# Gathering the first 32 edge blocks from x and looking their factors up by products

## What is computed

```python
def gcn_residual(x, edge_index, edge_weight, W, b, gamma, beta):
    deg = segment_sum(edge_weight, dst) + 1.0
    dinv = rsqrt(deg)
    norm = dinv[src] * edge_weight * dinv[dst]
    agg = segment_sum(norm[:, None] * (x @ W)[src], dst)
    agg = agg + (dinv * dinv)[:, None] * (x @ W)
    h = layernorm(agg + b) * gamma + beta
    return relu(0.5 * h + 0.5 * x)

xn = layernorm(x)
x = x + gcn_residual(xn, ...) + linear_attention(xn, Wq, Wkv, Wproj, bproj)
x = x + mixture_of_experts(layernorm(x))     # 16 experts, top 2
```

## Time and profile before

| | |
|---|---|
| median of three runs | 1661.91 us (1657.16 to 1662.6) |
| profiled execution | 1661.33 us |
| its span | 1659.5 us |
| busy in the span: PE, weight loads, DVE, ACT, POOL | 84%, 73%, 60%, 32%, 61% |
| first and last gather issued | 119.2 and 1105.2 us |

### The profile page before, as it was taken

One profiled execution on the slowest core, in us unless ns is written; L12 is line 12 of the kernel. 1 busy time (PEld: TensorE's weight loads), 2 busy tenths in 40 slices (PEclk: granted clock), 3 DMA queues, 4 the chain that ended last, 5 costly groups with the idle time before them and its releaser, 6 DMA issues. The chain is left out here.

```text
span 1659.5 us, 31767 instructions
## 1 busy us (share of the span) xinstructions
PE 1400.5 (84%) x8109; PEld 1212.2 (73%) x8110; DVE 999.2 (60%) x3840; ACT 525.4 (32%) x1448; POOL 1016.7 (61%) x1074
## 2 busy tenths in 40 slices
PE   5988987697797978787797789775899999999986
PEld 4777876586685867676686677663689999989974
DVE  7766564352774746547575277267655555566668
ACT  1474321121232222212222122013444444444424
POOL 0117777777777777777777777750345554545547
PEclk7889999997899879898899989786899999999998
DMA  8165433333333333333333333328532332254267
GB/s 278 30 201 151 124 106 106 103 105 105 105 105 105 105 105 105 105 106 103 105 105 105 105 105 106 105 74 156 156 121 73 97 100 96 81 170 152 74 232 280
DMA packets 110401, 201.27 MB, mean 121 GB/s; under 512 B 24880, under 2 KB 66480, under 8 KB 110288
## 3 DMA queue, kind: packets, MB, share of 16 engines
q0 software_dynamic: 48240, 131.91, 27.3%
q1 hardware_dynamic: 52704, 58.94, 11.7%
q10 hardware_dynamic: 9344, 9.05, 1.7%
HBM read 166.21 MB, written 33.60 MB: 120 GB/s over the span
## 5 line engine op out<-in xcount | busy, mean ns | idle before, releaser
L144 POOL DMA_INDIRECT ring<-table,src x782 | 748.8, 958 | 261.8 <-issue 221.3
L1273 PE MATMUL bank<-ring,work 128*128 x1756 | 432.3, 402 | 101.5 <-SPq L537 89.5
L1273 PEld LDWEIGHTS bank<-ring,work 128*128 128x128 f32 x1756 | 345.1, 200 | 178.1 <-issue 130.3
L1831 ACT ACTIVATE one<-bank,b 128x128 f32<-128x128 f32 x424 | 155.9, 368 | 217.3 <-PE bank L1858 192.3
L1858 PEld LDWEIGHTS bank<-one,w 128*128 128x128 f32 x1696 | 206.9, 193 | 8.1 <-issue 2.0
L1777 POOL DMA_INDIRECT spread<-y,to_x x109 | 109.1, 1001 | 163.1 <-DMA spread<-y,to_x 78.9
L1858 PE MATMUL bank<-one,w 128*128 128x128 f32 x1696 | 207.8, 276 | 1.2 <-issue 0.7
L1866 PE MATMUL bank<-w,one 128*128 128x256 f32 x848 | 201.5, 381 | 3.5 <-DVE y L1930 3.5
L756 DVE TENSOR_SCALAR work<-work 128x128 f32<-128x128 f32 x686 | 183.6, 365 | 2.0 <-DVE work L753 0.2
L1866 PEld LDWEIGHTS bank<-w,one 128*128 128x128 f32 x848 | 153.1, 191 | 20.5 <-issue 4.0
L774 DVE TENSOR_SCALAR work<-work,dst,w 128x128 f32<-128x128 f32 x192 | 58.2, 364 | 166.4 <-PE bank L1273 121.5
(11 more groups left out here) (303 smaller groups left out, 2136.7 us busy)
## 6 DMA issues: line engine op xcount, KB each, us to landing
w<-in_w SPq DMA_DIRECT2D x32, 512.0 KB, 4.8
ring<-table,src POOLq DMA_INDIRECT x782, 2.8
got<-spread SPq DMA_DIRECT2D x11, 1024.0 KB, 9.2
rows<-xn SPq DMA_DIRECT2D x1, 6272.0 KB, 27.1
out<-xn SPq DMA_DIRECT2D x12, 512.0 KB, 5.3
x<-in_x SPq DMA_DIRECT2D x4, 896.0 KB, 8.7
work<-in_x_cols ACTq DMA_DIRECT2D x28, 128.0 KB, 2.4
work<-in_x_cols SPq DMA_DIRECT2D x21, 128.0 KB, 3.2
```

What stands on the lines that cost most here:

```text
L144: return pool.indirect_dma_start(out=m.ring[:, b % RING, :], out_offset=None, in_=a.table, in_offset=bass.IndirectOffsetOnAxis(ap=m.src[:, ...
L1273: last = nc.tensor.matmul(agg, hot[:, k, :], two[:, k, :], start=False, stop=False)
L1831: act.activation(hT[:, fc, :], up_ps[fc], ACT.Relu, bias=b1[:, fc, bass.ds(i * SLOTS + slot, 1)]).then_inc(h_ok, 1)
```

## The change

The first 32 blocks (`GATHERED_AHEAD`) are gathered from x itself and no longer from the table. POOL does so as soon as the source indices have landed, which SP now loads right after the constants. Their rows lack the factor of their source node, so the factor is multiplied into the edge weights: during batches 2 to 9 DVE builds one-hots of the source's lane (`source_hots`), PE turns them (`sources`), ACT copies them out; DVE builds masks of the source's tile (`masks`). When the factors of all rows are known, DVE splits them into three bf16 parts (`split`), PE multiplies (`looked_up`, four groups of 24 matmuls), and DVE picks and sums (`found`) between the steps of the pair words.

The table's rows are now x times one factor, with no shift, since the weights of the graph layer are centred too. ACT takes the column sums out of PSUM and POOL adds them to the weights after its 32 gathers. The factor is the root of degree times variance in one. ACT scales and stores all tiles of the table, the last eight in two halves behind the lookups.

No keys are done during the histogram. All 49 tiles' keys come after the pair words, and eight tiles are visited among them, after the keys of tiles 1, 3, 9, 16, 23, 30, 37 and 44. The mixing visits 41 tiles and pauses in ten turns instead of five. POOL's gathers from block 32 on wait for the table and, as before, for freed slots. `summed_up` of the last tile comes in the turn after it. The statistics of x are taken two tiles a batch; x_cols are loaded later. The one-hots of the histogram no longer lie in the ring.

```diff
-TAIL = 16
-PAUSES = (8, 16, 24, 32, 40)
+PAUSES = tuple(range(0, 46, 5))
+TWICE = 2
+SOUGHT = 4
+SEEK = 8
...
+            pool.wait_ge(ld_src, 16)
             for b in range(GATHERED_AHEAD):
-                gather(pool, m, a, b).then_inc(landed[b // 4], 16)
+                gather(pool, m, a.x, b).then_inc(landed[b // 4], 16)
+            pool.wait_ge(seek_copied, CSUM_COPIED)
+            for ch in range(DC):
+                for k in range(3):
+                    w = m.weights[:, ch, k * D:(k + 1) * D]
+                    last = pool.tensor_tensor(w, w, csum[:, k * D:(k + 1) * D], ALU.add)
+            last.then_inc(read, 1)
...
+            pool.wait_ge(table_sent, 16 * (FINAL + 2))
             for b in range(GATHERED_AHEAD, FULL):
                 if b >= RING and b % 2 == 0:
                     pool.wait_ge(freed, (b + 2 - RING) // 2 + CREDIT)
-                gather(pool, m, a, b).then_inc(landed[b % RING // 4], 16)
+                gather(pool, m, a.table, b).then_inc(landed[b % RING // 4], 16)
...
-        VISITS_AFTER = {TAIL + 16: 0, TAIL + 23: 1, TAIL + 30: 2}
+        VISITS_AFTER = {1: 0, 3: 1, 9: 2, 16: 3, 23: 4, 30: 5, 37: 6, 44: 7}
...
+            def source_hots(k):
+                g0, g1 = k * SOUGHT // 2, (k + 1) * SOUGHT // 2
+                full = [P, g1 - g0, P, 2]
+                dve.tensor_tensor(src_hots[:, g0:g1], iota2[:, None, :, :].broadcast_to(full),
+                                  src_lo[:, 2 * g0:2 * g1].rearrange("p (g k) -> p g k", k=2)[:, :, None, :].broadcast_to(full),
+                                  ALU.is_equal).then_inc(seek_ok, 1)
...
+            def found(j):
+                b0, b1 = j * SEEK, (j + 1) * SEEK
+                dve.wait_ge(seek_mm, TURNED + 1 + j)
+                c.add(dve.tensor_tensor(sought[:, b0:b1].rearrange("p (g k) n -> p g k n", k=2),
+                                        found_ps[j].rearrange("p (g k) n -> p g k n", k=2),
+                                        src_mask[:, b0 // 2:b1 // 2].rearrange("p g n k -> p g k n"), ALU.mult))
+                c.wait()
+                c.add(dve.reduce_sum(s_edge[:, b0:b1], sought[:, b0:b1], axis=AX.X))
+                c.wait()
+                c.add(dve.tensor_tensor(m.w[:, b0:b1], m.w[:, b0:b1], s_edge[:, b0:b1], ALU.mult))
+                dve.sem_inc(seek_ok, 1)
...
+            for t, end, groups in ((t0, t0 + 4, FOUND // 2), (t0 + 4, t1, FOUND)):
+                act.wait_ge(seek_mm, TURNED + groups)
+                for of in range(t, end):
+                    scaled(of)
+                sent(t, end)
...
+            def looked_up(j):
+                for i in range(SEEK):
+                    b = j * SEEK + i
+                    for part in range(3):
+                        last = nc.tensor.matmul(found_ps[j][:, i, :], src_cols[:, b * P:(b + 1) * P], s_parts[:, part, :],
+                                                start=(part == 0), stop=(part == 2))
+                last.then_inc(seek_mm, 1)
...
-            for t in range(TAIL, NT):
+            pe.wait_ge(seek_ok, LOOKED)
+            pe.wait_ge(read, CENTRED_OK)
+            for t in range(NT):
                 scored(t)
-                context(t - 2)
+                if t >= 2:
+                    context(t - 2)
...
-                if on(t, 1) and not (t == LAST + 1):
+                if on(t, 1):
                     summed_up(t - 1)
```

More of the change, by code:

```diff
@@ L669, in scales @@
-                dve.wait_ge(rstd_ok, len(PARTS) + part)
-                c.add(root(m.dinv[:, t0:t1], var_p[:, t0:t1], seed_p[:, t0:t1], t1 - t0))
-                c.wait()
-                dve.tensor_tensor(row_scale[:, t0:t1], m.dinv[:, t0:t1], rstd[:, t0:t1], ALU.mult)
-                dve.tensor_tensor(row_shift[:, t0:t1], m.dinv[:, t0:t1], shift[:, t0:t1], ALU.mult).then_inc(rstd_ok, 1)
-            def centre():
-                dve.wait_ge(made, CSUM)
-                for k, (w0, n) in enumerate(CENTRED):
-                    for ch in range(DC):
-                        last = dve.scalar_tensor_tensor(m.weights[:, ch, w0:w0 + n], csum_ps[k], -1.0 / D, m.weights[:, ch, w0:w0 + n],
-                                                        ALU.mult, ALU.add)
-                last.then_inc(read, 1)
@@ L683, in _ @@
[L683 to L704 removed]
+                dve.wait_ge(seed_p_ok, SEEDED if part == FINAL else part + 1)
@@ L797, in aggregated @@
                 r.end()
-            between()
+            dve.wait_ge(read, CENTRED_OK)
             c.add(dve.tensor_copy(m.dst[:, 0:NB], dst_i))
@@ L811, in _, with seen @@
             dve.wait_ge(flag_ok, 1)
-            pair_words(dve, c, m, sums_ps, tf, between)
-            keys_to(FLAG_AFTER)
+            steps = iter(range(2 * FOUND + 3))
+            def seen():
+                step = next(steps)
+                if step % 2 == 1 and step // 2 < FOUND:
+                    found(step // 2)
+            pair_words(dve, c, m, sums_ps, tf, seen)
             with dve.If(out_of_order(dve)):
@@ new lines, in _ @@
+            for part in range(FINAL):
+                act.wait_ge(var_p_ok, part + 1)
+                seeds(part, grown, ln_s, seed_p, *DEGREES[part])
+                if part == 0:
+                    act.wait_ge(made, CSUM)
+                    act.activation(csum[:, 0:2 * D], csum_ps[0], ACT.Copy, scale=-1.0 / D)
+                    act.activation(csum[:, 2 * D:3 * D], csum_ps[1], ACT.Copy, scale=-1.0 / D).then_inc(seek_copied, 1)
+                if part == FINAL - 1:
+                    seeds(FINAL, var_p, spread, seed_x, 0, NT)
+                act.wait_ge(scale_ok, part + 1)
+                t0, t1 = DEGREES[part]
+                for t in range(t0, t1):
+                    scaled(t)
+                sent(t0, t1)
@@ new lines, in looked_up @@
+            def looked_up(j):
[4 more added lines that the diff above has]
+                                                start=(part == 0), stop=(part == 2))
+                last.then_inc(seek_mm, 1)
+            for b in range(BATCHES):
+                degrees(b)
+                if 3 <= b < 3 + TURNED:
+                    sources(b - 3)
+                if b == 3 + TURNED:
+                    column_sums()
@@ L1341, in _ @@
             pe.wait_ge(part_read, FINAL + 1)
             to_lanes(FINAL)
-            for t in range(TAIL, NT):
+            pe.wait_ge(ready, 2)
+            pe.wait_ge(var_p_ok, FINAL + 1)
+            for up in range(UP):
+                nc.tensor.matmul(sums_ps, m.ones[0:LOW], deg[:, 2, up::UP], start=(up == 0), stop=(up == UP - 1))
+            nc.tensor.matmul(drops_ps, m.ones, drops[:], start=True, stop=True).then_inc(made, 1)
+            pe.wait_ge(seek_ok, SPLIT)
+            pe.wait_ge(seek_copied, TURNED)
```

373 lines of the change are left out of this document (172 added, 201 removed).

## The result

| | before | changed |
|---|---|---|
| median (range) | 1662.26 us (1657.16 to 1663.57, 4 runs) | 1634.51 us (1633.52 to 1637.61, 4 runs) |
| profiled execution: time, span | 1661.33, 1659.5 us | 1635.0, 1633.2 us |
| first gather from the table, last gather | 119.2, 1105.2 us | 119.70, 1071.2 us |
| last visit ends | 1116.57 us | 1088.78 us |

The ratio is 0.9849 [0.9821, 0.9878]: 1.5% faster; the profiled executions lie 26.3 us apart, the medians 27.8. The forecast of 1625 us was 10 us too low; the time lies in the range of 1608 to 1650.

What follows compares the result with a forecast made beforehand. Serial gather stream on POOL bounds the kernel; last gather at 117 + 945.6 + 5 = 1067.6 us against 1105.2, 37.6 earlier, less 1 for the last sum; 1661.3 - 36.6 = 1624.7, about 1625 us; range 1608 to 1650.

Steps and rivals of the forecast that it cites:

- What bounds the kernel: Whole kernel: one serial stream of indirect gathers on POOL, 1.2625 us each; 986 of 1659.5 us hang on it.
- Part 1: Head: 32 gathers read x during the histogram, at most 1.57 us each, ending at 70 us; 750 left take 945.6 us.
- Rival A: Head is late: gathers crawl beside one-hots, weights come late or small steps grow; first gather about 135, 1643 us; chance 0.15.
- Part 2: Histogram without keys: one-hots end at 86 us against 98.97 (bounds 84 and 99), flag at 95 us against 117.4.
- Part 3: Pair words, lookups, first visit at 116 us, first gather into a freed slot at 117; bounds 115 and 130.
- Part 4: All 49 keys beside eight visits: PE runs against the stream, and POOL waits about 5 us near visit 8.
- Rival B: Keys stage: the ring stays full, a stall of 20 us and not 5, 1640 us; chance 0.14.
- Part 5: Mixing with ten pauses instead of five: PE's chain takes 729 us where the stream needs 824, so pauses stay hidden.
- rival C: Mixing: PE becomes the bound through pauses of 45.2 us with their visit; 1685 us at eight of ten; chance 0.07.
- D: Better than forecast: head at 110 us, no stall, PE not behind at the end, 1612 us; chance 0.09.
- The tail: After the last gather: last visit begins 5 us after its issue, left unchanged; bounds 6 us less, 12 us more.
- The last sum: End of the mixing: the last sum, one turn later, stands beside the last tile's aggregation and costs 1 us.

Runs made afterwards that it cites:

- the repeated run: The changed kernel itself run once more, nothing edited, beside the kernel before at 1662.61 us: 1636.98 us median, ratio 0.9837.
- the second group: Four runs at the usual time (kernel before 1662.61 us): changed kernel again 1636.98, 32 gathers from the table 1655.29, more PE work 1640.39, last five pauses earlier 1631.99 us.
- the third group: Four runs of edited changed kernels in slow executions, kernel before 2135.87 us; the one with the last sum back inside its visit took 2174.11 us, ratio 1.0196.

## Why the prediction was right where it was, and where it was off

**What bounds the kernel**: right. Putting 32 gathers back into the stream moved the time by 18.3 us for a last gather 18.7 us later, and products added to PE, which made it 17.4 us busier, moved it by 3.4.

**Part 1, the cover of the early gathers**: held, with a wrong bound. The row gave at most 1.57 us; during the histogram the median was 1.485 and the longest 2.790 us (`L146 POOL DMA_INDIRECT ring<-in_x,src x32` above; 1.266 and 2.787 in the repeated run). Two gathers with next to nothing on DVE beside them took the usual time, so reading x is not what made the others slow:

```profile
46.98 0.94 POOL L146 DMA_INDIRECT ring<-in_x,src  x1 [0.30 <-issue]
48.22 0.94 POOL L146 DMA_INDIRECT ring<-in_x,src  x1 [0.30 <-issue]
```

The 32 still ended at 66.6 us, inside the 70 expected: (65.6 - 7.7) / 31 = 1.87 us from one to the next, which is what 1.57 + 0.30 had allowed. The 109 us that I had worked out by the Trainium skill's figure (SBUF — State Buffer, the single rule of contention) did not come; nor did 3100 ns show in any gather. Rival A's slow gathers exist, up to 2.79 us each, and are hidden behind the histogram.

**Part 2**: one-hots ended at 86.7 (predicted 86), the flag came at 95.14 (95), and at 96.33 to 98.59 in the second group's executions.

**Part 3**: first visit at 116.85 (116). The four lookups took 1.37 us each (1.35), and the products 4.16 us (7, bounds 3.6 to 12.5): 43 ns each, close to the nearer row. The lookups' products ran at a granted clock of 0.52. The term that was off is small: one microsecond from the visit's start to the first gather. It took 2.85 us, all of it PE's matmuls at a granted clock of 0.50:

```profile
116.80:119.70 2.90, 2.85 (x7) 2.33 (x8) 2.09 (x10) 0.00 (x0) 0.00 (x0) 0.50 0.01 3
```

With the visit itself 0.85 us late that makes 119.7 in place of 117, **+2.7 us**.

**Part 4**: the turns were 21.5 us, PE was the later one, and the ring-full stall at visit 8 was 4.94 us (5 taken). It has its row:

```profile
282.71 1.15 POOL L146 DMA_INDIRECT ring<-table,src  x1 [4.94 <-PE bank L1298]
```

A second one, of 2.91 us at 328.99, followed the pause at turn 0; the sum had none there. In all the 749 gathers took 951.5 us against 945.6 + 5 = 950.6, **+0.9 us**. Rival B (a stall of 20 us) did not come.

**Part 5**: but for the 2.91 us at turn 0 the pauses stayed hidden up to turn 40, as predicted: POOL's rate in the windows is 1.25 us a gather. Three of them took 33, 42 and 41 us where 28.9 was usual. Together that is 29 us more, as much as 1.8 of rival C's long pauses, where 4.2 would have decided (the 4.3 of the prediction, worked out again). What the prediction had wrong about C is its nature: it took the one pause of 45.2 us for something that befalls one pause in five at a low clock. The traces show that it goes with the tile. Of the tiles from 8 on, six (9, 13, 23, 30, 40 and 46) have 40 weight loads in their visit and the others 36 or fewer, so the six have a pair of blocks more. In the kernel before, five of them had no pause in front, and from the row of the tile before to their own they took 25.0 to 30.9 us, where no other visit without a pause took over 22. Two of the five, tile 30 with 757.64 - 728.76 = 28.9 us and tile 46 with 30.9:

```profile
728.76 0.47 ACT L1132 ACTIVATE xn<-bank,dinv 128x256 f32<-128x256 f32 x1 [1.96 <-PE bank L1320]
757.64 0.45 ACT L1132 ACTIVATE xn<-bank,dinv 128x256 f32<-128x256 f32 x1
...
1054.25 0.47 ACT L1132 ACTIVATE xn<-bank,dinv 128x256 f32<-128x256 f32 x1 [8.81 <-PE bank L1320]
1085.14 0.45 ACT L1132 ACTIVATE xn<-bank,dinv 128x256 f32<-128x256 f32 x1
```

The pause of 45.2 us stood before the sixth, tile 13. The changed kernel's pauses at turns 25 and 45 stand before tiles 30 and 46, and these are the 42 and the 41 us, in the repeated run too (41.3 and 41.1); the 33 us are tile 14, right behind tile 13. So the long rows are the price of a pause on top of a visit that is long anyway. With the pauses moved, tile 46 took 1058.48 - 1027.29 = 31.2 us. The granted clock does not tell the two cases apart: it was 0.78 in the kernel before from 1054.25 to 1085.14 and 0.76 in the changed one from 1019.17 to 1059.99. Why one pair more costs so much was not followed up. Behind the pause at turn 45 only three visits are left in which to catch up.

**The tail**: this is the term that was mis-sized. I left it as it was, 11.4 us from the last gather to the last visit's end, and had 12 us more as a bound "if a pause at turn 45 leaves it behind". It did: 17.6 us, **+6.2**, and the run with earlier pauses shows that the place of the pauses is the cause, since it took the distance to 8.2 us and the time down by 5.0 although its stream ended later.

**The last sum**: from the last visit's end to the routing's first step on DVE went 16.3 us where it was 14.4, so **+0.9** over the 1 us predicted. The time from the visit's end to DVE's first step on its result went from 2.77 to 4.59 us, which is nearly all of it. Only the traces say so, as the run that undid it fell in the third group.

Sum: 1624.7 + 2.7 + 0.9 + 6.2 + 0.9 = 1635.4 us, against 1635.0 in the profiled execution; from the routing's first step on it took 0.4 us less than the kernel before. That the range held is in part luck: it was laid out for D, A and B, none of which came, and what used most of its room was the tail, whose bound of 12 us was stated but not added to the range.

## What to carry to other kernels

Find the serial stream that everything behind it waits for, and price a change by how many of its instructions leave it and when it can start; an engine's share of busy time did not tell this here. When a stream is shortened by a few per cent, look at once at what was second: here it was PE's chain in the last turns, and moving planned gaps away from the end of the stage and from its longest visits gave 5 us for one line. When one row of ten is long, ask first which piece of the data it works on: the rows of the kernel before already had the long visits. A gain that comes from a shorter stream is a gain only while that stream is the bound: in executions in which the engines stood still for other reasons, kernels with the same change were slower than the kernel before.

## What the runs showed of the hardware that was not expected

An indirect gather issued from POOL during the histogram, beside DVE's 16-bit one-hots and its row statistics, took up to 2.79 us and 1.485 us in the median (1.266 in the repeated run), where it takes 0.946 us in the median behind it. More matmuls in PE's gaps went with a higher granted clock, 0.920 in place of 0.908, so that products of 42 us or more made PE only 17.4 us busier and cost 3.4 us. And the same kernel can take 28% longer in a whole group of runs, with every kernel beside it, gathers of unchanged duration and idle times of 5 to 14 us that the profile puts down to nothing it knows.
